# A macaron block on one core: slot sums in products of 512 columns, exponentials between tiles, more weights loaded during attention, fewer final transfers

## The reference

```python
x = x + 0.5 * moe(layernorm(x))         # layer 0
x = x + attention(layernorm(x))         # 16 heads of 128, 4 groups of keys and values
x = x + 0.5 * moe(layernorm(x))         # layer 1, the same weights as layer 0

def moe(x, router_w, w1, v1, w2):       # 64 experts, top 8, 96 hidden features, 32 slots each
    probs = softmax(x @ router_w.T); wts, idx = top_k(probs, 8); wts = wts / sum(wts)
    # a token's copy goes to its expert's next free slot; past 32 it is dropped
    h = silu(einsum('ecd,efd->ecf', xg, w1)) * einsum('ecd,efd->ecf', xg, v1)
    y = einsum('ecf,efd->ecd', h, w2)
    # each slot's row, times its weight, is added to its token's row
```

## Time and profile before

| | us |
|---|---|
| median of 3 runs | 657.53 (656.26 to 657.68) |
| the profiled execution | 657.74 |
| its span | 655.9 |
| TensorE busy | 623.6 (95%) |
| VectorE busy | 504.9 (77%) |
| ScalarE busy | 386.0 (59%) |
| GpSimd busy | 52.2 (8%) |

### The profile page before, as it was taken

How to read it: one execution, slowest core, us unless ns; L and a number is a source line. 1 busy time by engine, 2 the same in 40 slices (tenths; PEclk the granted TensorE clock), 3 DMA queues, 4 the chain that set the end, 5 groups by cost and what they waited for, 6 DMA issues and landing times.

```text
span 655.9 us, 12187 instructions
## 1 busy us (share of the span) xinstructions
PE 623.6 (95%) x4572; PEld 536.4 (82%) x4572; DVE 504.9 (77%) x1316; ACT 386.0 (59%) x1048; POOL 52.2 (8%) x75
## 2 busy tenths in 40 slices
PE   8589989999999999999999999999999998997995
PEld 6367777999889999999889999989899997774774
DVE  6836668889997778889777788877788888694663
ACT  5724476677666655666665666656566665581442
POOL 3343000000000000000000000000000000034310
PEclk9779999999999999999999999999999999977998
DMA  8999870000000000000000000000000007175993
GB/s 315 338 412 418 307 263 1 2 1 1 0 1 1 1 1 1 0 1 1 1 1 1 1 0 1 1 1 1 1 0 1 1 11 311 36 270 182 420 397 105
DMA packets 27621, 62.53 MB, mean 95 GB/s; under 512 B 7014, under 2 KB 17382, under 8 KB 27558
## 3 DMA queue, kind: packets, MB, share of 16 engines
q1 hardware_dynamic: 25398, 55.97, 22.6%
q0 software_dynamic: 1664, 5.30, 2.1%
q10 hardware_dynamic: 496, 0.43, 0.3%
HBM read 54.34 MB, written 7.34 MB: 94 GB/s over the span
## 4 chain that ended last, share of the span: by engine, by line
PE 77%; DVE 10%; DMA 7%; ACT 2%; issue 1%; SPq 1%; POOL 0%; another core or an unknown queue 0%; POOLq 0%; DVEq 0%
PE bank L1401 19%; PE bank L1403 19%; PE bank L1402 19%; PE bank L1457 8%; PE bank L1243 3%; PE bank L1201 3%; DMA wo_raw<-wo_in 2%; DMA down_r<-down_in 2%; PE bank L1253 2%; PE bank L1173 1%; DMA slots<-token_table,slot_index 1%; DMA x<-x_in 1%; DVE probsT_lo L1101 1%; DVE negmax L1066 1%; DVE ln L806 1%
## 5 line engine op out<-in xcount | busy, mean ns | idle before, releaser
L718 ACT ACTIVATE probs<-bank,negmax 128x256 f32<-128x256 f32 x256 | 121.4, 494 | 0.7 <-DVE negmax L1066 0.6
L726 ACT CAST probsT_hi<-bank 128x512 fp32r<-128x512 f32 x128 | 68.7, 590 | 71.0 <-PE bank L1457 71.0
L701 ACT ACTIVATE o_hi<-bank,bv 128x512 fp32r<-128x512 f32 x64 | 44.2, 690 | 66.7 <-PE bank L1403 66.7
L1101 DVE TENSOR_TENSOR probsT_lo<-bank,probsT_hi 128x512 fp32r<-128x512 f32 x128 | 81.8, 680 | 0.5 <-ACT probsT_hi L726 0.5
L1066 DVE TENSOR_REDUCE negmax<-bank 128x2 f32<-128x512 f32 x128 | 81.7, 680 | 0.0
L1074 DVE TENSOR_SCALAR probs<-probs,rowinv 128x256 f32<-128x256 f32 x256 | 73.1, 349 | 2.3
L1401 PE MATMUL bank<-wo_hi,o_hi 128*128 128x256 f32 x256 | 73.1, 285 | 0.0
L1403 PE MATMUL bank<-wo_hi,o_lo 128*128 128x256 f32 x256 | 72.6, 284 | 0.0
L1403 PE MATMUL bank<-k_hi,q_lo 128*128 128x256 f32 x256 | 72.4, 283 | 0.0
L1402 PE MATMUL bank<-k_lo,q_hi 128*128 128x256 f32 x256 | 72.4, 283 | 0.0
L1402 PE MATMUL bank<-wo_lo,o_hi 128*128 128x256 f32 x256 | 72.3, 282 | 0.0
(11 more groups left out here) (181 smaller groups left out, 1342.7 us busy)
## 6 DMA issues: line engine op xcount, KB each, us to landing
up_r<-up_in SPq DMA_DIRECT2D x16, 768.0 KB
down_r<-down_in SPq DMA_DIRECT2D x14, 512.0 KB
up_q<-up_in SPq DMA_DIRECT2D x8, 768.0 KB, 8.8
up_o<-up_in SPq DMA_DIRECT2D x6, 768.0 KB
down_q<-down_in SPq DMA_DIRECT2D x8, 512.0 KB, 9.6
token_table<-xn SPq DMA_DIRECT2D x16, 256.0 KB, 2.4
down_o<-down_in SPq DMA_DIRECT2D x6, 512.0 KB
x<-x_in SPq DMA_DIRECT2D x4, 512.0 KB, 5.6
```

Source lines behind the costliest of these rows:

```text
L701: nc.scalar.activation(dst, src, ACT.Identity, bias=bias).then_inc(work_high, 1)
L718: nc.scalar.activation(probs[:, n % 2, t, :], scores_ps[head][:, qt * S:qt * S + S], ACT.Exp, bias=negmax[:, n % 2, t:t + 1], accum_out=ro ...
L726: nc.scalar.copy(probsT[0][:, head].rearrange("p c s -> p (c s)"), probsT_ps[head][:]).then_inc(probsT_high, 1)
L1101: nc.vector.tensor_tensor(probsT[1][:, head].rearrange("p c s -> p (c s)"), probsT_ps[head][:], probsT[0][:, head].rearrange("p c s -> p ( ...
```

## The change

1. **Slot sums.** High and low part of a group's outputs lie side by side, and one product of 512 columns takes both; a bank holds one block of 128 tokens with the high sums in its left half and the low sums in its right. The wide sums take four banks instead of two (2, 3, 6, 7), `narrow_ps` is bank 5. The transposed hidden values move from bank 2 to bank 0, behind the transposed slots, the down products to bank 4. Two waits come with that on TensorE: the transpose of hidden waits for the copy of the next group's slots, and the first down product for the limit.
2. **Halves added.** ScalarE copies a bank's left half into `stage` (`copy_high_sums`), VectorE adds the right half: after layer 0 into x (`finish_tokens`, 8 additions), the first pair before the statistics and the others between the first fills; after layer 1 in place (`add_low_sums`, 5 additions).
3. **Start of attention.** ScalarE's splits 6 to 11 are spread over later fills; 16 idle products instead of 20.
4. **Router of layer 1.** The exponentials come after 4 and 6 tiles (before: both after 12), the table is stored in another order.
5. **Loads.** Seven groups of layer 1 instead of four are loaded before attention ends, two then, three after the first gathers. For that the homes r are four separate buffers, and q and k have buffers for even and odd groups of heads.
6. **Final transfers.** Two wide ones of 256 KB instead of four of 128 KB; the narrow ones are shared out 3, 4 and 1 instead of 3, 3 and 2 (SyncE, GpSimd, ScalarE).

```diff
-            homes_r = homes(moe, "r", 4)
+            homes_r = [home for n in range(4) for home in homes(moe, f"r{n}_", 1)]
...
+        wide_ps, narrow_ps, down_ps, idle_ps = bank[2:4] + bank[6:8], bank[5], bank[4], bank[1]
...
+        def stage_of(n):
+            return stage[:, n // 2, D * (n % 2):D * (n % 2) + D]
...
-        def store_wide(engine, n, odd):
+        def store_wide(engine, odd):
...
             def store_table(layer):
                 store_tokens(0)
-                store_tokens(1)
+                if layer == 0:
+                    store_tokens(1)
+                store_weights(0)
                 if layer == 1:
-                    store_tokens(2)
-                store_weights(0)
+                    store_tokens(1)
+                    store_weights(1)
+                store_tokens(2)
                 if layer == 0:
-                    store_tokens(2)
                     store_weights(1)
                 store_tokens(3)
-                if layer == 1:
-                    store_weights(1)
...
-            for g in range(len(homes_q)):
+            for g in range(len(homes_q) + 3):
                 load(1, g)
             sp.wait_ge(attention_done, 1)
-            for g in range(len(homes_q), 6):
+            for g in range(len(homes_q) + 3, 9):
                 load(1, g)
...
-                first = TILES - 4 if layer == 1 else TILES // 2
-                normalise(0, first)
+                stops = ((8, 8), (4, 6))[layer]
+                normalise(0, stops[0])
                 for h in range(2):
                     act.wait_ge(scaled_ready, 2 * layer + h + 1)
                     nc.scalar.activation(expw[:, 8 * h:8 * h + 8, :], expw[:, 8 * h:8 * h + 8, :], ACT.Exp).then_inc(exps, 1)
+                    if h == 0:
+                        normalise(*stops)
                 act.wait_ge(moments_ready, 2 * layer + 1)
-                normalise(first, TILES)
+                normalise(stops[1], TILES)
...
+                    copy_high_sums(PAIRS, narrow_stage, narrow_ps)
+                    for n in range(PAIRS):
+                        copy_high_sums(PAIRS + 1 + n, stage_of(n), wide_ps[n])
+                    act.wait_ge(staged[0], 2)
+                    act.wait_ge(staged[1], 2)
+                    store_wide(nc.scalar, 1)
+                    store_narrow(nc.scalar, B - 1)
+
+            def copy_high_sums(seen, dst, sums):
+                act.wait_ge(bank_summed, seen + 1)
+                nc.scalar.copy(dst, sums[:, 0:D]).then_inc(high_copied, 1)
...
+            for n in range(PAIRS):
+                copy_high_sums(n, stage_of(n), wide_ps[n])
+            for n in range(4, 6):
+                split_high(n)
...
             for n, job in enumerate(first_fills):
+                if n == 5:
+                    act.wait_ge(x_final, PAIRS)
                 take_fill(*job)
-                if 1 <= n < 5:
-                    split_high(n + 7)
+                if 1 <= n < 6:
+                    split_high(n + 5)
+                if n == len(first_fills) - 1:
+                    split_high(11)
...
+            def add_low_sums(seen, dst, sums, done):
+                dve.wait_ge(high_copied, seen + 1)
+                nc.vector.tensor_tensor(dst, dst, sums[:, D:2 * D], ALU.add).then_inc(done, 1)
+
+            def finish_tokens(n):
+
+                dve.wait_ge(high_copied, n + 1)
+                for odd in range(2):
+                    rows = slice(WIDE * odd, WIDE * odd + WIDE)
+                    last = nc.vector.tensor_tensor(x[0:WIDE, 2 * (2 * n + odd), :], stage_of(n)[rows, :], wide_ps[n][rows, D:2 * D], ALU.add)
+                last.then_inc(x_final, 1)
...
                 marks = onehot[:, s % MARKS, :]
+                parts = y_parts[:, s, :, :].rearrange("p l d -> p (l d)")
                 if layer == 1:
-                    for low in range(2):
-                        last = mm(bank[5][:, 0:D], marks[:, RANGE:FIRST[1]], y_parts[:, s, low, :], start=False,
-                                  stop=final and low == 1, skip_group_check=True)
+                    last = mm(narrow_ps[:], marks[:, RANGE:FIRST[1]], parts, start=False, stop=final, skip_group_check=True)
                     if final:
                         last.then_inc(bank_summed, 1)
-                for n in range(2):
-                    for low in range(2):
-                        last = sum_wide(bank[6:8], n, marks, y_parts[:, s, low, :], False, final and low == 1)
+                for n in range(PAIRS):
+                    last = mm(wide_ps[n][:], marks[:, n * P:n * P + P], parts, start=False, stop=final, skip_group_check=True)
...
                 if s > 0:
+                    if s + 1 < GROUPS:
+                        pe.wait_ge(slotsT_ready, sT_seen.now() + 1)
                     pe.wait_ge(hidden_ready, hidden_seen.add())
-                    nc.tensor.transpose(bank[2][0:F, 0:P], hidden[:],
+                    nc.tensor.transpose(bank[0][0:F, KD * P:KD * P + P], hidden[:],
                                         ident[:]).then_inc(hiddenT_raw, 1)
...
+                    if s == 1:
+                        pe.wait_ge(limit_ready, layer + 1)
...
-                    keep_busy(20)
+                    keep_busy(16)
```

More of the change, by code:

```diff
@@ L33 @@
 PARTS = B // 2
+PAIRS = B // 2
 GROUPS_OF_TOKENS = T // B
@@ L450, in _ @@
             wait_for_gathers(1)
-            for g in range(6, AHEAD):
+            for g in range(9, AHEAD):
                 load(1, g)
@@ L544, in _ @@
             pool.wait_ge(staged[2], 1)
-            for b in range(3, 6):
+            for b in range(3, 7):
                 store_narrow(nc.gpsimd, b, narrow_stored)
@@ L1335, in expert_layer @@
                 if layer == 0:
-                    take_tokens()
+                    take_tokens(layer)
                 else:
```

109 lines of the change are left out of this document (49 added, 60 removed).

## The result

| | us |
|---|---|
| kernel before, median of 13 runs | 659.24 (656.26 to 661.79) |
| changed kernel, median of 13 runs | 664.82 (659.66 to 667.56) |
| ratio, changed to before | 1.0075, 95% interval 1.0055 to 1.0096 |
| changed kernel, profiled execution | 666.05, span 664.0, granted clock 0.965 |

The forecast was 657.1, range 653.9 to 659.4, and none of the three rivals reached the measured time. The ratio is worth 4.9 us. The two profiled executions lie 8.1 us apart in span, in part since that of the kernel before ran 1.5 us under its median and that of the change 1.2 above; that sum can be followed. I cut both at four marks: the first idle product behind the last sums of layer 0, the first v product, GpSimd's first operation at the end of attention, and the first gather of layer 1.

What follows compares the result with a forecast made beforehand. The prediction took TensorE's products to bound the steady slot steps, with no weight waited for. Its terms, +0.9 -1.5 +1.2 -0.4 -0.6 = -0.4 us, gave 657.3 on the profiled execution, 657.1 against the median, range 653.9 to 659.4.

Steps and rivals of the forecast that it cites:

- the start of attention: After layer 0: VectorE's adds and later sums delay the first v product by 0.9 us, to 99.5; bounds -0.3 and +3.4.
- Waits of layer 0 and 1, "+1.2" each: Steps 1 and 2 of each layer: hidden's transpose waits for ScalarE's slots copy, adding 1.2 us per layer.
- the clock, a side remark of the forecast: First slot steps of layer 1: a clock rising at the same moment returns up to 0.9 us; later, bound 2.8.
- Router, "-1.5": Router of layer 1: earlier exponentials free VectorE of GpSimd, returning 2.1 us; first gather 1.5 us earlier; bounds -2.1 and 0.
- Land 2.2 later: Router of layer 1: the last table rows, issued by 589.2, land 2.2 us later, at 591.4 to 591.7.
- rival 3: Router of layer 1: rows for the gather land late, so it gains nothing; total +1.1, 658.6 us; chance 0.12.
- the forecast of -0.4: Whole kernel: the terms sum to -0.4 us, 657.3 on the profiled execution, 657.1 against the median.
- Sums of 512 columns, "-0.4": Slot steps of layer 1: merged pairs save 0.025 us a group, 0.4 over 16 groups; bounds 0 and 1.5.
- Loads, 0: Layer 1 weights: three more groups loaded before attention ends gain 0, since TensorE waited for no weight.
- End, "-0.6": Last stores: later sums, but fewer ScalarE transfers, end the kernel 0.6 us earlier; bounds -1.2 and +0.9.
- Rival 1: First slot steps of layer 1: ScalarE's idle stretch closes; total -2.0 to -4.5, between them -3.3, 654.2 us; chance 0.22.
- Rival 2: Start of attention: VectorE becomes the bound, +3.4 instead of +0.9; total +2.1, 659.6 us; chance 0.18.

Runs made afterwards that it cites:

- e1: Changed kernel with TensorE's 16 idle products at the end of layer 0 moved behind the branch over the late ranges: 659.55 us, ratio to before 1.0021.
- e11: Kernel before with 67 more idle products in the never-entered body of the late ranges of layer 0: 662.99 us, ratio to before 1.0072.
- e2: Changed kernel with 8 more idle products in the never-entered body of the late ranges of layer 0: 662.06 us (one run), ratio to before 1.0063.
- e4: e1 with hidden of layer 0 transposed into its own bank, without the wait for the slots copy there: 658.54 us, ratio to before 1.0000.
- e5: Kernel before with only the wait for the next group's slots copy added ahead of hidden's transpose: 657.93 us, ratio to before 0.9998.
- e3: Kernel before with only the router's part of the change (exponentials after 4 and 6 tiles, new table order): 656.78 us, ratio to before 0.9988.
- e7: e4 with more idle products in layer 1 (28 for 16, then 6) and its first exponential after 5 tiles: 657.68 us, ratio to before 0.9988.
- e8: e1 with the change's loads undone, four groups of layer 1 loaded during attention instead of seven: 660.13 us, ratio to before 1.0028.
- e9: e7 with fewer additional idle products in layer 1 (22 instead of 28, 3 instead of 6): 661.20 us, ratio to before 1.0033.

## Why the prediction was wrong

**The step that failed** is the start of attention: "+0.9" there, with bounds "-0.3" and "+3.4". Measured, the first v product starts 6.8 us later in the change, 2.2 of them ahead of the idle products and 4.6 behind. The step counted the work of the engines and put nothing down for the arrival of TensorE's instructions. The changed program puts other instructions at the end of a block, and that cost 3.6 us by the median of e1 against the change; e11, with the jump itself beyond the blocks, lost 4.7 against before. I had weighed every instruction that runs and none that is only jumped over. The profile of before held a hint, hard to read ahead of the result: two 16 KB instruction packets starting at 88.0 and 92.8, beside this branch, and a gap put down to "issue" ahead of the first transposes:

```profile
90.50 1.09 PE L1424 MATMUL bank<-ident,xn 128*128 128x128 f32 x8 [0.40 <-issue]
```

Where the instructions arrive in time the order of VectorE is the one that the step walked through, but the number is right by luck. e1 has the first v product at 99.86, forecast 99.5. The forecast had layer 0 end 0.9 later and the rest take as long as before; e1 ended layer 0 at the same time as before (85.5) and took 1.2 longer behind it. Over all profiles without the fetch gap the stretch is 12.6 to 13.8 on the side of the kernel before and 13.7 to 14.4 on that of the change, 0.9 apart in the mean.

The Trainium skill ("Runtime: NRT & Kernel Launch", section "Instruction fetch mechanics") says that instructions are fetched in blocks of 16 KiB, one ahead, and that a taken branch whose target lies outside the two blocks at hand forces a fetch before anything runs. The trace agrees, with 16 KB packets and gaps of 4.9 and 5.0 us at the jump in e11 and e2. The change shows a milder case, told by its trace alone: three transposes run and then 2.9 us of nothing, and from the end of the work ahead of the jump to the restart it is 4.7 us, about as in the other two. In all three, and in the kernel before, a packet of this queue starts 2.5 to 2.7 us behind the end of that work, which fits a fetch that is asked for at the jump.

**Waits of layer 0 and 1, "+1.2" each** (that of layer 0 inside the "+0.9"). The place was right in layer 0 (steps 1 and 2, nowhere else), and at full clock so was the size: 1.15 us between e1 and e4. What the step had wrong is that this reaches the end: e5 has 0.9998 with an upper end of 1.0017, where 2.4 us would be 1.0036, and in e4 a later gather and an idle stretch ahead of the last down products take the gain of doing without the waits back. In the profile of the change the clock, a side remark of the forecast, stayed at half until 47 us in layer 0 and 617 in layer 1 (before: 43.6 and 606.8), and layer 0 ended 2.2 later.

**Router, "-1.5".** VectorE's part was right (0.17 and 0.29, index 1.6 nearer). "Land 2.2 later" failed: with ten tiles behind the exponentials, the last of four row stores takes 3.5. That is rival 3, given 0.12: 0 in the change, 0.7 in e3, 0.8 with one tile more ahead (e7). A busy queue alone doesn't explain it: the DMA share was 1.00 to 1.17 in e1 from 588 to 592, and 1.02 to 1.20 in the kernel before from 588 to 591, where the last row store took 2.4. Why it is 2.4, 2.8 and 3.5 isn't settled; e8 excludes the loads.

Of the 5.3 us between the forecast of -0.4 and the measured +4.9, the fetch is 3.6 by e1 and the router's missing gain 1.5 on paper (an estimate from profiles); what is left is below what the medians can tell.

**Sums of 512 columns, "-0.4".** Right: 2.86 against 2.88 a step, 0.2325 us a product. **Loads, 0.** Right (e8). **End, "-0.6".** -0.5 in the pair of profiles; but from the last but one group's first wide or narrow sum to the end, the six profiles on the side of before have 9.4 to 10.0 us and the eight of the change 8.9 to 10.3, with means of 9.7 and 9.6. A gain isn't shown.

**Rivals.** Rival 1 (ScalarE's stretch closes) did come about in nine of fourteen profiles, but not in that of the change, and the stretch isn't the change's: e7 and e9 have the same ScalarE program, one without it and one with. So the rival's condition changes from one execution to the next, or with what other engines do; its cause is open. Its price was of the right size: from the first gather to the end, profiles without the stretch are 2.2 us shorter in the mean (rival 1 had 1.55 without the clock). Rival 2 (VectorE as the bound) did not happen: behind the idle products, without the fetch gap, it is 0.9 us more in the mean and 1.3 at most, not its 3.4.

**What stays open:** 1.4 us between e1 and the kernel before (its interval reaches from -0.3 to 3.2), of which the profile puts 1.2 at the start of attention; whether the waits keep the clock low; the landing of 3.5 us; ScalarE's stretch; why e9 is slower than e7. No run jumps beside an idle DMA queue, so how much of the 4.7 to 5.0 us is the other transfers isn't known.

## What to carry to other kernels

Where an engine runs a branch over code that is seldom entered, look where its target falls in the instruction blocks: here 67 products that never run cost 0.72% (e11). A gap with no releaser on the engine that jumped, with the others idle soon after and an instruction packet in it, is the sign; work that needs no data, put behind the jump, covered the fetch and gave back 0.54% (e1). When the store that a gather waits for is the last of many, count its landing from the slowest in the trace, not from the median. And ahead of pricing a wait in a stage that starts a layer, compare several profiles: the granted clock there differs between them, and a wait that shows in the first steps can be taken back by a later one.

## What was not expected of the hardware

- Sixty-seven products that never run cost 4.7 us (e11, interval 3.0 to 6.5), more than the whole change was expected to bring.
- From the end of the work ahead of the jump to the first instruction behind it: 5.01 us in e2, 4.87 in e11; in the change 4.71 to the first one behind the gap. The clock was at its lower level (1.2 GHz) for some 5 us behind the gap in the change.
- Of the last four row stores of the change, 256 KB each, the third lands in 2.1 us and the fourth, issued 0.4 later, in 3.5 (3.4 to 3.6 in e1, e2, e4 and e8, 3.0 in e7 and e9); in the order of before the last one takes 2.4.
- ScalarE idles 2.0 to 2.6 us, put down to no engine of the profile, at most once or twice in a run and only in the first slot steps of layer 1, in five of fourteen profiles.
